# Queries projected transposed and placed by DMA, and score-maxima units moved among the routers, in a fused cross-attention and routed-FFN kernel

## The chip, the cores and the metric

The kernel runs on one core of a Trainium2 chip. The metric is the device time of one execution in microseconds (us), as the median of three runs; lower is better. PE is TensorE, DVE is VectorE, ACT is ScalarE, POOL is GpSimd and SP is SyncE, which issues most of the DMAs.

## The reference, cut to what matters

`x` is (4, 1024, 256), the context is (4, 154, 256), all in float32. With LN a layer norm without weights:

```
q = (LN(x) @ Wq.T + bq) * 16**-0.5     16 heads of 16 dims
k = ctx @ Wk.T + bk ; v = ctx @ Wv.T + bv
q, k = xpos(q), xpos(k)                pairs of dims rotated by position
x1 = x + tanh(g0) * (softmax(q k.T) v) @ Wo.T + bo   (bo inside the tanh factor)
h  = relu(mole(LN(x1), W1, b1, A1, B1, R1))          256 -> 1024
y  = x1 + tanh(g1) * mole(h, W2, b2, A2, B2, R2)     1024 -> 256
mole(x) = x @ W + b + 1/8 * sum over 3 experts of gate_e * (x @ A_e) @ B_e
gates   = softmax(x @ R)
```

The rotation turns each pair (x1, x2) of neighbouring dims into x1 cos - x2 sin and x2 cos + x1 sin.

## The kernel before, in words

**Steps.** The 4096 tokens are worked in 8 steps of 512 tokens (`CH`); step c covers half of one batch element, c = 2b + u. Each engine has its own program, written out by hand in `step`: steps 0 and 1 are special (`first`, `second`), steps 2 to 5 are a loop of two iterations, and steps 6 and 7 are written out again, with a tail behind them. The engines are kept together only by semaphores, and each works its own queue strictly in order. A step c works on three chunks of tokens at once: attention of c, the first FFN layer of d = c - 1, and the second FFN layer of e = c - 2. Steps 2 to 7, which hold all three, are called full.

**Number format.** Products that need full precision are made of float32r matmuls, with each operand split in a high and a low part and three products summed.

**Order of one full step on PE** (lines 1178 to 1258): the key operands if u is 0 (`key_transposes`, `project_v`); `out_tile` 0 and 1 of e (24 matmuls each, L1112); `project_out` of d (L988); `lora2_operand`, `out_tile` 2 and 3; `transpose_x`, which transposes the normalised rows of d into PSUM banks 2 and 3 of `psX` (L943); the first two groups of `q_transposes` of c (L1085); `lora2_operand` (L1122), `router1` of d (32 small matmuls, L1028), `out_lora` (L1128); then groups 2 to 7 of `q_transposes`, with `hidden_main(d, 0)` in two halves between them; `lora1_operand` (L1037), the transposed gated operand of layer one. Then come 16 units of `max_scores` (L1099, two matmuls of 308 columns each). Behind each of the first 13 stands half a `hidden_main` (three matmuls of 512 columns, L1052), and behind each second half the `hidden_lora` (L1058) that ends the sum of a hidden block of 128. After the tenth unit (i = 9) comes `max_transposed` (L1139). Last are 10 `scores` steps (L1155, L1158) with `values` (L1172, L1175), the transposes and `project_q` (L970) of c + 1 among them.

**Queries before.** `project_q` makes q with tokens on partitions: 24 matmuls of 256 columns. DVE adds the bias (`q_bias`, L646, 2 instructions), POOL multiplies by the cosines (L323), DVE by the sines (`q_sine`, L653, 4 instructions) and adds (`q_sum`, L661). ACT copies the high part twice into `split` (two 128x1024 copies), DVE subtracts it for the low part (`q_low`, L678). PE transposes 8 groups of two heads (32 transposes, 96 rows: high, low, high), and the groups are copied out of PSUM into `qT`, four by ACT and four by DVE (`q_transposed`, L721).

**The part around the maxima.** `reduce_max(c, i)` on DVE (L733) takes the maxima of unit i out of `psX`; unit i + 2 uses the same two banks, so `max_scores(c, i)` waits for reduction i - 2. `relu(d, m)` on ACT (L431) follows `hidden_lora(d, m)`, and `h_low(d, m)` on DVE (L726) follows `relu(d, m)`. There are three PSUM banks for hidden blocks, so `hidden_main(d, m)` waits for `h_low(d, m - 3)`. On ACT, `maxima_copy(c)` (L433 to L436) stands between `relu(d, 3)` and `relu(d, 4)`. It waits for `max_transposed(c, 0)`, which waits for eight reductions. `scores(c, 0)` waits for reduction 14. On DVE the order is two reductions, one `h_low`, and so on, so that ten reductions stand ahead of `h_low(d, 4)`:

```
for i in range(16):
    reduce_max(c, i)
    if not first:
        if i % 2:
            h_low(d, i // 2)
```

**Queues.** SP issues the loads at the start, and then only `rows_of_maxima`: four DMAs of 8 KB per step, from `split` into rows 96 and 97 of `qT`. ACT issues the x and context loads and the stores.

Of the kernel before, what the change touches and what calls it, by code (L numbers as in the profile page):

```python
# [65 lines left out]
def build(nc, x, ctx_in, wq, wkv, wo, w1, w2, a1, lora, tables, out):  # L66
    with ExitStack() as stack:
# [14 lines left out]
        split = sb("split", [P, TT * NG * KS], F32R)  # L82
        qs = split[:, :].rearrange("p (k g r) -> p k g r", k=TT, g=NG)
# [10 lines left out]
        q_ev = probs[:, 0:2, :].rearrange("p a (k e) -> p (a k) e", e=E)  # L94
        q_rc = probs[:, 2:4, :].rearrange("p a (k e) -> p (a k) e", e=E)
        q_rs = probs[:, 4:6, :].rearrange("p a (k e) -> p (a k) e", e=E)
# [18 lines left out]
        tab = sb("tab", [P, tables.shape[1]])  # L115
        ident_r = sb("ident_r", [P, P], F32R)
# [29 lines left out]
        cos_q = cols(UB * TT * D).rearrange("p (u k d) -> p u k d", u=UB, k=TT)  # L146
        sin_q = cols(UB * TT * D).rearrange("p (u k d) -> p u k d", u=UB, k=TT)
        cos_k = cols(2 * D).rearrange("p (a d) -> p a d", a=2)
        sin_k = cols(2 * D).rearrange("p (a d) -> p a d", a=2)
        bq_b, bk_b, bv_b, bo_b = cols(E), cols(E), cols(E), cols(E)  # L150
        g_b, mask = cols(2), cols(2)
# [34 lines left out]
        q_ps, q_evac = count("q_ps", 2), count("q_evac", 2)  # L186
        q_cos, q_sin, q_rot = count("q_cos", 1), count("q_sin", TT), count("q_rot", 1)
        q_hi, q_hi2, q_lo = count("q_hi", 1), count("q_hi2", 1), count("q_lo", 1)
        qT_ps, qT_a, qT_v = count("qT_ps", NG), count("qT_a", NG // 2), count("qT_v", NG // 2)
# [52 lines left out]
        def _(sp):  # L242
# [5 lines left out]
            stage("wq", wq)  # L248
            sp.dma_start(tab[:, :], tables).then_inc(tab_loaded.sem, 16)
# [13 lines left out]

            def rows_of_maxima(c):
# [7 lines left out]

            rows_of_maxima(0)
            rows_of_maxima(1)
            with sp.Fori(1, B) as b:
                rows_of_maxima(2 * b)
                rows_of_maxima(2 * b + 1)
# [3 lines left out]
        def _(pool):  # L281
# [37 lines left out]
            def step(b, u, first=False, last=False):  # L319
                c = 2 * b + u  # L320

                pool.wait_ge(q_evac.sem, q_evac.at(c))
# [31 lines left out]
        def _(act):  # L354
# [100 lines left out]
            def step(b, u, first=False, second=False, last=False):  # L455
# [5 lines left out]
                if first:  # L461
                    load(0, 1, 1)
                if u == 0:
                    key_operands(b)
# [6 lines left out]
                if not first:  # L471
                    act.wait_ge(wo_ps.sem, wo_ps.at(d))
# [908 lines left out]
```

## Time and profile before

| | us |
|---|---|
| median of 3 runs | 614.66 |
| lowest and highest run | 612.47, 615.61 |
| the profiled execution | 608.41 |
| its span, first to last instruction | 606.6 |
| mean granted TensorE clock | 0.946 |

The profile shows one execution. Busy times are the time in which an engine had an instruction in work. A group of instructions is named by the line that issues them, the tile written and the tile read. In a row of a timeline stand the start, the time from the first start to the last end, the engine, line and operation, the tiles and shapes, and in brackets how long the engine had been idle before it and who ended that.

The steps end, by the start of the next `project_q`, at 75.2, 141.5, 208.4, 275.0, 344.2, 410.9 and 477.5 us; what is behind step 7 begins at 543.5 us.

### The profile page before, as it was taken

Reading aid. Unit: us, or ns where it says so; the run is one execution under the profiler, and the core shown is the slowest. Engines: PE = TensorE matmul, PEld = TensorE weight load, DVE = VectorE, ACT = ScalarE, POOL = GpSimd, SP = SyncE. Lnnn points to the kernel's source line nnn. Section 1 sums busy time; section 2 is a strip of 40 time slices with the busy share of each in tenths; the row PEclk is TensorE's granted clock in tenths of the full one; section 3 lists DMA queues with packets and bytes.
Section 4 is the critical chain, followed back from the end, with each engine's and each line's share of the span. In section 5 each row is a group of like instructions: output and inputs, shape, how many; then the busy total and the mean of one; then the engine's idle time right before and its main releaser. Section 6 shows DMA issues by size and latency. Waiting matters only on the chain.

```text
span 606.6 us, 9214 instructions
## 1 busy us (share of the span) xinstructions
PE 527.2 (87%) x3360; PEld 400.8 (66%) x3360; DVE 415.7 (69%) x960; ACT 239.3 (39%) x389; POOL 84.8 (14%) x121
## 2 busy tenths in 40 slices
PE   2668965999989998999989998999899998989795
PEld 1545454856977497746876497747886597649574
DVE  4567356958887487956987487958897578644423
ACT  3252514453345424362445424362436343442210
POOL 2426012011100121011201121011201110101000
PEclk9865977999999998999999998999999999999798
DMA  8301000010001000010001010111001000100000
GB/s 263 111 2 36 2 35 2 1 47 27 11 2 72 1 36 2 36 47 10 31 1 72 1 36 2 41 42 37 1 1 71 1 2 1 71 1 1 1 36 35
DMA packets 6138, 18.57 MB, mean 31 GB/s; under 512 B 932, under 2 KB 1772, under 8 KB 5964
## 3 DMA queue, kind: packets, MB, share of 16 engines
q10 hardware_dynamic: 4005, 12.53, 5.8%
q1 hardware_dynamic: 2087, 5.42, 2.7%
q8 instruction: 29, 0.48, 0.3%
q14 instruction: 17, 0.14, 0.1%
HBM read 13.49 MB, written 4.19 MB: 29 GB/s over the span
## 4 chain that ended last, share of the span: by engine, by line
PE 68%; DVE 16%; ACT 7%; issue 6%; ACTq 1%; POOL 1%; DMA 1%; DVEq 0%
PE psF L1112 16%; PE psF L1052 11%; PE psX L1099 6%; ACT probs L521 5%; PE psX L1158 4%; DVE max_t L733 4%; PE psX L988 4%; PE psX L970 4%; PE psO L1172 3%; PE psO L1175 3%; PE psF L1172 3%; PE psF L1175 2%; PE psX L1085 2%; PE psF L1058 2%; PE psF L1028 1%
## 5 line engine op out<-in xcount | busy, mean ns | idle before, releaser
L733 DVE TENSOR_REDUCE max_t<-psX 128x4 fp32r<-128x616 f32 x128 | 99.5, 794 | 6.5 <-PE psX L1099 3.3
L521 ACT ACTIVATE probs<-psX 128x1024 f32<-128x1024 f32 x64 | 64.0, 1024 | 50.8 <-PE psX L1158 50.8
L1112 PE MATMUL psF<-w_hi,h_hi 128*128 128x284 f32 x256 | 76.8, 300 | 2.4 <-DVE h_lo L726 1.5
L1112 PE MATMUL psF<-w_lo,h_hi 128*128 128x284 f32 x256 | 75.1, 293 | 0.0
L1112 PE MATMUL psF<-w_hi,h_lo 128*128 128x284 f32 x256 | 74.9, 293 | 0.0
L1099 PE MATMUL psX<-km,qT 96*128 96x308 f32 x256 | 65.1, 341 | 6.9 <-DVE max_t L733 4.5
L1099 PEld LDWEIGHTS psX<-km,qT 96*128 96x128 f32 x256 | 48.6, 204 | 23.5 <-DVE max_t L733 12.8
L431 ACT ACTIVATE h_hi<-psF 128x512 fp32r<-128x512 f32 x64 | 37.3, 595 | 62.4 <-PE psF L1058 62.1
L726 DVE SCALAR_TENSOR_TENSOR h_lo<-psF,h_hi 128x512 fp32r<-128x512 f32 x64 | 43.7, 684 | 16.3 <-ACT h_hi L431 16.3
L1112 PEld LDWEIGHTS psF<-w_hi,h_hi 128*128 128x128 f32 x256 | 48.2, 188 | 7.9 <-issue 4.6
L1052 PE MATMUL psF<-xT_lo,w_hi 128*128 128x512 f32 x128 | 51.6, 414 | 0.0
L311 POOL TENSOR_TENSOR x<-x,tab 128x256 f32<-128x256 f32 x32 | 22.3, 730 | 206.4 <-DMA x<-in_x_dram 206.4
L1158 PE MATMUL psX<-qT,km 98*128 98x512 f32 x128 | 45.0, 447 | 4.6 <-ACT probs L521 4.1
L1112 PEld LDWEIGHTS psF<-w_hi,h_lo 128*128 128x128 f32 x256 | 48.2, 188 | 0.0
L1112 PEld LDWEIGHTS psF<-w_lo,h_hi 128*128 128x128 f32 x256 | 48.2, 188 | 0.0
L1052 PE MATMUL psF<-xT_hi,w_hi 128*128 128x512 f32 x128 | 42.8, 417 | 1.0 <-DVE zc L783 1.0
L1158 PEld LDWEIGHTS psX<-qT,km 98*128 98x128 f32 x128 | 20.5, 195 | 33.1 <-issue 17.2
L1052 PE MATMUL psF<-xT_hi,w_lo 128*128 128x512 f32 x128 | 40.6, 399 | 0.0
L757 DVE STREAM_TRANSPOSE heads_t<-psF 128x512 f32<-128x512 f32 x16 | 11.5, 717 | 38.5 <-PE psF L1175 33.8
L323 POOL TENSOR_TENSOR probs<-probs,tab 128x1024 f32<-128x1024 f32 x8 | 18.9, 2367 | 106.9 <-DVE probs L646 106.9
L1085 PE MATMUL psX<-ident_r,split 128*96 128x128 f32 x256 | 25.2, 253 | 4.9 <-DVE split L678 4.9
L356 ACT ACTIVATE split<-heads_t 128x512 fp32r<-128x512 f32 x16 | 10.0, 626 | 48.6 <-DVE heads_t L772 48.6
(155 smaller groups left out, 1003.4 us busy)
## 6 DMA issues: line engine op xcount, KB each, us to landing
x<-in_x_dram ACTq DMA_DIRECT2D x8, 512.0 KB, 3.3
x_ln<-in_x_dram ACTq DMA_DIRECT2D x7, 512.0 KB, 3.2
out_dram<-x ACTq DMA_DIRECT2D x7, 512.0 KB, 2.7
heads_t<-in_w_dram SPq DMA_DIRECT2D x1, 1024.0 KB, 8.3
heads_t<-in_w_dram SPq DMA_DIRECT2D x1, 994.0 KB, 4.7
tab<-in_tables_dram SPq DMA_DIRECT2D x1, 674.0 KB, 6.8
x_ln<-in_x_dram SPq DMA_DIRECT2D x1, 512.0 KB, 3.4
wkv_sb<-in_wkv_dram SPq DMA_DIRECT2D x1, 512.0 KB, 9.7
```

The lines of the kernel that those rows point to most:

```text
L431: nc.scalar.activation(h_hi[:, m, :], psF[:, (m + 1) % 3, :], ACT.Relu).then_inc(w1_hi_s.sem, 1)
L521: nc.scalar.activation(dst, psX[:, 2 * (i % 2):2 * (i % 2) + 2, :], ACT.Exp).then_inc(sc_exp.sem, 1)
L726: V.scalar_tensor_tensor(out=h_lo[:, m, :], in0=psF[:, (m + 1) % 3, :], scalar=0.0, in1=h_hi[:, m, :].bitcast(F32), op0=ALU.max, op1=ALU.s ...
L733: V.tensor_reduce(max_t[:, k, half, :].rearrange("p (h g) -> p g h", h=2)[:, 2 * j:2 * j + 2, :], psX[:, 2 * j:2 * j + 2, 0:2 * S].rearran ...
L970: ins = mm(o_ps, a[:, f, tokens(k)], w[:, f, :], start=n == 0, stop=n == 5)
L1052: mm(psF[:, (m + 1) % 3, :], w[:, f, P * m:P * m + P], a[:, f, :], start=n == 0, stop=False)
L1085: ins = nc.tensor.transpose(psX[0:KS, g % 4, tokens(k)].bitcast(F32R), qs[:, k, g, :], ident_r[:, :])
L1099: ins = mm(psX[:, g % 4, 0:2 * S], qT[0:KS, g, tokens(k)], km[0:KS, g, :, :].rearrange("p h s -> p (h s)"), start=True, stop=True)
L1112: ins = mm(psF[:, F_OF_K[k], 0:W2N], a[:, m, tokens(k)], w[:, m, :], start=m == 0 and i == 0, stop=m == HT - 1 and i == 2)
L1158: ins = mm(o_ps, km[:, n // 2, j, 0:P], qT[:, n // 2, :], start=True, stop=True)
L1172: mm(pv_bank(g), vr_sb[:, g, :], probs_r[:, g, :], start=True, stop=False)
L1175: ins = mm(pv_bank(g)[32 * j:32 * j + 32, :], v_sb[:, h, :], probs[:, h % 8, :], start=False, stop=True)
```

## The change

It does five things.

1. `project_q` swaps its operands: the weights are stationary, the tokens move. q comes out transposed, as two banks `psX[:, s, :]` of 128 rows by 512 tokens (12 matmuls of 512 columns). The weights are permuted so that bank 0 holds the first dim of each pair, bank 1 the second.
2. The rotation is done there. DVE makes four products with bias and table in one instruction each (`q_products`) and one difference and one sum of 128x512 (`q_turn`). ACT copies the high part (2 x 128x512) and DVE makes the low part (`q_low`, 2 x 128x512). POOL has no part in it any more. The tables of a half (512 KB) are loaded by SP for every step (`next_turn`).
3. Six DMAs of 256 KB per step on the SP queue put the rows in place in `qT`. They read 128 partitions by 2 KB and write 16 partitions by 16 KB. All PE transposes of q and the eight copies out of PSUM are gone.
4. The order of the maxima changes on PE and DVE, by `maxima_and_hidden`. In full steps unit 0 stands ahead of the router, unit 1 behind it, and the other 14 stand 2, 2, 2, 2, 3, 3 to the hidden blocks 2 to 7. Hidden blocks 0, 1 and 2 go ahead of `lora1_operand`. In step 1 six units go ahead of the transposes of x.
5. In step 0, `q_low` stands ahead of `key_operands`. On ACT the copies of the high part stand behind the first x load and ahead of `key_operands`.

```
+            def rows_of_queries(c):
+                for s in range(2):
+                    sp.wait_ge(q_hi.sem, q_hi.at(c, s + 1))
+                    for t in (0, 64):
+                        sp.dma_start(qT[t + 16 * s:t + 16 * s + 16, :, :].bitcast(F32),
+                                     probs[:, 4 + s, :]).then_inc(q_rows.sem, 16)
+                for s in range(2):
+                    sp.wait_ge(q_lo.sem, q_lo.at(c, s + 1))
+                    sp.dma_start(qT[32 + 16 * s:48 + 16 * s, :, :].bitcast(F32),
+                                 probs[:, s, :]).then_inc(q_rows.sem, 16)
+            def next_turn(c, u):
+                sp.wait_ge(q_prod.sem, q_prod.at(c))
+                sp.dma_start(turn[:, :, :], turns[u]).then_inc(turn_loaded.sem, 16)
...
+            def q_products(c):
+                dve.wait_ge(turn_loaded.sem, turn_loaded.at(c))
+                for s in range(2):
+                    dve.wait_ge(q_ps.sem, q_ps.at(c, s + 1))
+                    for dst, w in ((q_c, s), (q_s, 1 - s)):
+                        V.scalar_tensor_tensor(out=dst[:, w, :], in0=psX[:, s, :], scalar=bq_c[:, s:s + 1],
+                                               in1=turn[:, w ^ s, :], op0=ALU.add, op1=ALU.mult).then_inc(q_prod.sem, 1)
...
DVE, step:
-                for i in range(16):
-                    reduce_max(c, i)
-                    if first and i == 5:
-                        ln1_stats(c + 1)
-                    if not first:
-                        if i % 2:
-                            h_low(d, i // 2)
+                    n = MAX_AHEAD if second else 0
+                    for i in range(n):
+                        reduce_max(c, i)
                     x2T_low(d)
+                    reduce_max(c, n)
                     gates1_shift(d)
+                    reduce_max(c, n + 1)
+                    if full:
+                        finish(e, u, 2)
+                        finish(e, u, 3)
                     gates1_weigh(d)
+                    h_low(d, 0)
+                    h_low(d, 1)
+                    i = n + 2
+                    for m in range(2, HT):
+                        for _ in range(max_units(m, second)):
+                            reduce_max(c, i)
+                            i += 1
+                        h_low(d, m)
...
PE:
+            def maxima_and_hidden(c, d, e, full, second):
+                n = MAX_AHEAD if second else 0
+                if second:
+                    pe.wait_ge(x1_s.sem, x1_s.at(d))
+                    for i in range(n):
+                        max_scores(c, i)
+                    pe.wait_ge(max_red.sem, max_red.at(c, n))
+                transpose_x(d, psX[:, 2:4, :], ln2_out, x2T_ps)
+                pe.wait_ge(x1_s.sem, x1_s.at(d))
+                max_scores(c, n)
+                if full:
+                    lora2_operand(e, 1)
+                router1(d, second)
+                if full:
+                    out_lora(e, 1)
+                max_scores(c, n + 1)
+                for m in range(3):
+                    hidden_main(d, m, second)
+                lora1_operand(d)
+                hidden_lora(d, 0)
+                hidden_lora(d, 1)
+                i = n + 2
+                for m in range(2, HT):
+                    k = max_units(m, second)
+                    for part in range(2):
+                        for _ in range(k // 2 if part else k - k // 2):
+                            max_scores(c, i)
+                            if i == 9:
+                                max_transposed(c, 0, False)
+                            i += 1
+                        if m >= 3:
+                            hidden_main(d, m, second, (part,))
+                    hidden_lora(d, m)
...
+MAX_AHEAD = 6
+def max_units(m, second):
+    return ((0, 0, 1, 1, 1, 1, 2, 2) if second else (0, 0, 2, 2, 2, 2, 3, 3))[m]
```

The wait of `max_scores(c, 0)` is now for `q_rows`, all six DMAs; the order of `relu` and `maxima_copy` on ACT is as before.

## Rows read from the trace of the kernel before

**Rows 1.** Page, part 1: busy us and share of the span of each engine.
```profile
PE 527.2 (87%) x3360; PEld 400.8 (66%) x3360; DVE 415.7 (69%) x960; ACT 239.3 (39%) x389; POOL 84.8 (14%) x121
```

**Rows 2.** Busy time by stretch: PE, PEld, DVE, ACT, POOL, granted clock, DMA share, GB/s.
```profile
41.00:56.70 15.70, 13.47 (x37) 8.39 (x37) 13.95 (x26) 6.63 (x11) 11.88 (x11) 0.50 0.11 34
...
368.90:375.10 6.20, 6.15 (x69) 5.36 (x69) 4.56 (x16) 1.65 (x4) 0.00 (x0) 0.72 0.00 0
...
443.60:461.60 18.00, 17.23 (x88) 14.17 (x87) 16.84 (x26) 7.18 (x14) 0.00 (x0) 1.00 0.08 31
```

**Rows 3.** Groups by line with shapes kept apart: busy us, mean ns, idle before.
```profile
L1085 PE MATMUL psX<-ident_r,split 128*96 128x128 f32 x256 | 25.2, 253 | 4.9 <-DVE split L678 4.9
...
L721 DVE CAST qT<-psX 96x512 fp32r<-96x512 f32 x32 | 21.7, 680 | 4.3 <-PE psX L1085 4.3
...
L646 DVE TENSOR_TENSOR probs<-psX,tab 128x512 f32<-128x512 f32 x16 | 11.0, 688 | 3.7 <-PE psX L970 3.6
...
L678 DVE TENSOR_TENSOR split<-probs,split 128x1024 fp32r<-128x1024 f32 x8 | 9.7, 1210 | 0.0
```

**Rows 4.** Timeline of PE in step 6, from the x transposes to the scores.
```profile
436.11 0.77 PE L1085 MATMUL psX<-ident_r,split 128*96 128x128 f32 x8
...
438.82 0.64 PE L1028 MATMUL psF<-xT_hi,a_sb 128*32 128x128 f32 x16 [0.96 <-DVE xT_lo L639]
...
440.17 0.69 PE L1085 MATMUL psX<-ident_r,split 128*96 128x128 f32 x8
...
443.29 0.45 PE L1037 MATMUL psO<-ident_r,zs 128*96 128x128 f32 x4
...
445.22 0.39 PE L1058 MATMUL psF<-zT,lora_sb 96*128 96x512 f32 x1
445.45 0.45 PE L1099 MATMUL psX<-km,qT 96*128 96x308 f32 x2
445.74 0.40 PE L1052 MATMUL psF<-xT_lo,w_hi 128*128 128x512 f32 x1
...
454.55 0.41 PE L1139 MATMUL psO<-ident_r,max_t 128*8 128x128 f32 x4
...
461.61 0.49 PE L1155 MATMUL psX<-qT,kr 98*128 98x512 f32 x1
```

**Rows 5.** Timeline of DVE in step 6.
```profile
418.32 1.39 DVE L653 TENSOR_TENSOR probs<-probs,tab 128x256 f32<-128x256 f32 x4
...
437.39 1.28 DVE L639 TENSOR_TENSOR xT_lo<-psX,xT_hi 128x512 fp32r<-128x512 f32 x2
...
446.65 0.68 DVE L726 SCALAR_TENSOR_TENSOR h_lo<-psF,h_hi 128x512 fp32r<-128x512 f32 x1
...
456.09 0.69 DVE L726 SCALAR_TENSOR_TENSOR h_lo<-psF,h_hi 128x512 fp32r<-128x512 f32 x1 [0.54 <-ACT h_hi L431]
456.69 1.50 DVE L733 TENSOR_REDUCE max_t<-psX 128x4 fp32r<-128x616 f32 x2
```

**Rows 6.** Timeline of ACT in step 6.
```profile
443.77 0.59 ACT L356 ACTIVATE zT<-psO 96x512 fp32r<-96x512 f32 x1
445.65 0.60 ACT L431 ACTIVATE h_hi<-psF 128x512 fp32r<-128x512 f32 x1 [1.28 <-PE psF L1058]
...
454.99 0.59 ACT L356 ACTIVATE split<-psO 8x512 fp32r<-8x512 f32 x1 [3.11 <-PE psO L1139]
```

**Rows 7.** Timeline of DVE and PE in steps 0 and 1.
```profile
33.93 1.41 DVE L710 TENSOR_SCALAR km<-psX,tab 98x512 fp32r<-98x512 f32 x2
...
41.05 7.03 PE L1099 MATMUL psX<-km,qT 96*128 96x308 f32 x16
...
97.78 1.97 PE L943 MATMUL psX<-ident_r,xn 128*128 128x128 f32 x8 [7.55 <-ACT xn L411]
```

**Rows 8.** Page, part 6: DMA issues, KB each, median us from issue to landing.
```profile
x_ln<-in_x_dram ACTq DMA_DIRECT2D x7, 512.0 KB, 3.2
...
out_dram<-x ACTq DMA_DIRECT2D x2, 256.0 KB, 2.1
```

More of the change, by code:

```diff
@@ L63, in at, with build @@
         return self.per * n + (self.per if k is None else k)
-def build(nc, x, ctx_in, wq, wkv, wo, w1, w2, a1, lora, tables, out):
+def build(nc, x, ctx_in, wq, wkv, wo, w1, w2, a1, lora, tables, turns, out):
     with ExitStack() as stack:
@@ L271, in rows_of_maxima, with step @@
                                      max_f[4 * hh:4 * hh + 4, f, :].bitcast(F32)).then_inc(max_rows[f].sem, 16)
[L273 to L277, printed above, removed]
+            def step(b, u, last=False):
+                c = 2 * b + u
+                rows_of_queries(c)
+                if not last:
+                    next_turn(c, 1 - u)
+                rows_of_maxima(c)
+            step(0, 0)
+            step(0, 1)
+            with sp.Fori(1, B - 1) as b:
+                step(b, 0)
+                step(b, 1)
+            step(B - 1, 0)
+            step(B - 1, 1, last=True)
         @block.gpsimd
@@ L462, in step @@
                     load(0, 1, 1)
+                if not first:
+                    act.wait_ge(pv_ps.sem, pv_ps.at(d))
+                for s in range(2):
+                    act.wait_ge(q_rot.sem, q_rot.at(c, s + 1))
+                    copy(qh[:, s, :], q_c[:, s, :]).then_inc(q_hi.sem, 1)
                 if u == 0:
@@ L481, in step @@
                     x2T_high(d)
-                for g in range(0, NG, 2):
-                    act.wait_ge(qT_ps.sem, qT_ps.at(c, g + 1))
-                    copy(qT[0:KS, g, :], psX[0:KS, g % 4, :]).then_inc(qT_a.sem, 1)
-                    if full and g == 0:
-                        gate2_copy(e, 1)
-                    if not first and g == 0:
-                        gate1_exp(d)
+                if full:
+                    gate2_copy(e, 1)
                 if not first:
+                    gate1_exp(d)
                     gate1_copy(d)
@@ L822, in step @@
                     finish(e, u, 1)
-                q_low(c)
                 if full:
@@ L964, in project_q @@
                     pe.wait_ge(w_lo["wq"].sem, 1)
-                for k in range(TT):
-                    o_ps = psX[:, k // 2, E * (k % 2):E * (k % 2) + E]
+                for s in range(2):
                     n = 0
```

211 lines of the change are left out of this document (72 added, 139 removed).

## The prediction

> **What bounds the kernel now.** I read the page's busy shares first: PE is busy for 87% of the span, DVE for 69% [rows 1]. That names PE, but not the place. So I read the stretches next. From the first hidden blocks to the scores of step 6 PE is busy 17.23 of 18.0 us and DVE 16.84 of 18.0 [rows 2]: in the part that the change rebuilds, the two are full together, and neither can go faster without the other. That stretch stands in each of the six full steps. Third, the timelines of step 6. I set the clock to zero where DVE has finished the low part of the transposed x, at 437.39 + 1.28 = 438.67 us [rows 5], because the router waits for that and nothing ahead of it changes: up to there PE works on out tiles that the change doesn't touch. From that zero, before: router 0.15, gated operand 4.62, first `hidden_lora` 6.55, first scores 22.94 [rows 4], first `h_low` 7.98 [rows 5].
>
> **What leaves and what comes.** PE loses 256 transposes, 25.2 us busy in all, 3.15 a step [rows 3]. Its projection is 12 times 512 columns for 24 times 256, the same column count, so I cost it at nothing. DVE loses four casts of 680 ns a step, two bias sums of 688 and a low part of 1210 [rows 3], the four sine products (1.39 us) [rows 5] and one sum about as long as the low part. It gains four products, two halves of the turn and two of the low part. Priced as 128x512 rows, the four products are 4 x 0.69 = 2.8 us where the bias took 1.4; the turn and the low part are about 1.2 us each. The products fall between `project_q` and the last values of the step, where DVE waits for PE, and the turn takes the place of the sine products. So the DVE saving that lies on the path is the four casts, 2.5 us. POOL's cosines go; nobody was behind them. ACT's copies go; ACT has slack throughout. The new tables are fetched by a 512 KB load, 3.2 us [rows 8], a step early; the work that hides it is the whole step.
>
> **The rows' DMAs.** Six of 256 KB a step. No row here writes few partitions with that much. Bounds: below, half a 512 KB load, 1.6 us each or 9.6 us for six; above, 3.2 us each, a whole load, or 19.2 us [rows 8]. I take 2.1 us, the row of the 256 KB store [rows 8], since it also reads SBUF and has the same size: 12.6 us one behind the other. In step 6 the turn ends near 418.3 + 1.3 = 419.6 [rows 5]; the rows start at 420.2 and end at 432.8. Unit 0 is wanted where the q transposes were, at 436.1 [rows 4]. So in full steps they cost nothing; their cover is PE's out tiles, 16 us of them, and beyond that all PE work stops behind unit 0, which now stands ahead of the router.
>
> The Trainium skill, SBUF — State Buffer, Door 1: The DMA port swizzle, says that a transfer's rate goes with the ports its partitions reach, and that partitions 0 to 15 reach four of sixteen, measured at 104 GB/s. By it a 256 KB piece would take an estimated 2.5 us and six 15 us, and the sum below would be about 6 us higher. No run here shows it yet. It also speaks against this change, since each piece writes 16 partitions.
>
> **A full step, after.** I follow the new queues from the same zero.
> - Router to 1.5, with its lora product behind it (PE is free for the next at 440.17 [rows 4]). Unit 1 takes 0.29, the step from 445.45 to 445.74 [rows 4]. Then three hidden blocks stand ahead of the gated operand: 18 matmuls of 0.23, the step from 445.22 to 445.45 [rows 4], 4.2 us. The operand comes at 6.0, against 4.62.
> - ACT's copy starts 0.48 after it and lasts 0.59 [rows 4, 6], so the first `hidden_lora` is at 7.1; relu 0.43 behind that, `h_low` 0.63 later: 8.2 against 7.98. The removed transposes have bought nothing by here, because what the gates wait for is no longer filled by them but by hidden work, and DVE stands idle from about 5.0, when its gates are done.
> - From the first `h_low` to the scores, before, 14.96 us. DVE's own work in it is 13 reductions of 0.70 (two take 1.50 with an overlap, 1.50 - 0.80 [rows 5]) and 7 `h_low` of 0.60 (from 456.09 to 456.69 [rows 5]), 13.3 us. The same 13 and 7 stand there after: only units 0 and 1 were done earlier, and they were before, too. So this stretch has no saving at all, only new gaps:
>  - `h_low(4)`. It waits for relu 4, that for `maxima_copy`, that for the maxima's transposes, those for the eighth reduction. From those transposes to the `h_low` is 456.09 - 454.55 = 1.54 us [rows 4, 5]. Before, ten reductions stood ahead of it, so two (1.4 us) filled the wait and 0.54 was left [rows 5]. After, eight stand ahead: none fills it. The eighth ends, PE finishes the half block in front (0.3) and unit 9 (0.3), then 1.54: a gap of 2.2. Price 1.7.
>  - Blocks 6 and 7 have three units each. The middle of each block now waits for a reduction of its own group, and `hidden_lora` and relu follow: 0.8 at `h_low(6)`, 0.5 at `h_low(3)`.
>  - At the end, unit 15 waits for reduction 13, and half a block (0.7) and its `hidden_lora` (0.2) stand between it and the scores: 0.6 more than before.
> - So 14.96 becomes 17.6 less the rounding of these, scores at 8.2 + 17.6 = 25.8, against 22.94: **2.9 us slower** a full step. Behind the scores the queues are as they were.
> - In two of the six steps the clock was down in the stretch behind the router (0.72, and 6.2 us for what takes 5 elsewhere [rows 2]). There 18 big matmuls now stand instead of 6, so I add 0.3 for each of two steps.
>
> Six full steps: 6 x 2.9 + 0.6 = +18.0.
>
> **Step 0.** Before, the maxima begin at 41.05 [rows 7]. After, `q_low` comes ahead of the key operands that began at 33.93 [rows 7], and ends at 35.2; the two low pieces take 4.2, so they land at 39.5: -1.5. (Bounds 38.4 and 41.6, so -2.7 to +0.6.) Loading the tables costs at the start: 512 KB in the SP queue ahead of the weights, hidden, since PE waits for the layer norm there.
>
> **Step 1.** Six units go ahead of the x transposes of 97.78, where PE had been idle for 7.55 us [rows 7]. A unit takes 0.88 there (16 matmuls, 8 units in 7.03 [rows 7]), 5.3 us. The rows start near 84 and land at 96.5; units to 102.3; transposes 4.5 late. Behind it six reductions less (4.2), given back by 1.2 where the first `h_low` comes later: -3.0. Sum +1.5. With the lower bound of the rows it is -1.
>
> **Sum.** 18.0 - 1.5 + 1.5 = +18.0: a span of 624.6 for 606.6, a profiled execution of 626.4 for 608.41. The profiled execution stands 6.2 us below the median of the runs, 614.66, so against that: 614.66 + 18.0 = **632.7 us**, 2.9% slower.
>
> **Rivals.**
> - *The gaps don't open, and the casts and transposes come off.* This needs DVE to be the pace with PE always ahead of it. For it: 16.84 of 18.0 busy [rows 2]. Then each full step gains its four casts, 2.5 us, steps 0 and 1 gain 1.5 and 1: 614.66 - 17.5 = 597; all PE transposes gone is the floor, 589.5. It decides when the first `h_low` comes by 5.5 from zero and the one at block 4 has no gap. Against it: the order of ACT and the eight reductions. Chance 0.22.
> - *Partly filled.* The gaps only eat the saving: 612 to 618. Chance 0.08.
> - *Rows late.* From 13.5 us for six, unit 0 holds up PE's queue. At 2.5 us each, between the row taken and the upper bound: step 0 +1.4 instead of -1.5, step 1 +3.9 more than at 2.1 less 1.5, i.e. +2.4, full steps 0.2 each: about +6, 639. At 3.2 each about 4 us a full step, 660. The mechanism is that each piece writes only 16 partitions, unlike every row above. Chance 0.22, the larger because nothing like it is in this trace. (The rule of the Trainium skill's page named above is this one.)
> - *The clock falls in the maxima.* In step 0, with maxima alone, PE is 13.47 of 15.7 busy and the clock stays at 0.50 [rows 2]. After, PE has gaps in the same stretch of each full step. At half clock its 36 big matmuls and 14 units take some 7 us more: 675. Against it, they are mixed with full-sized matmuls. Chance 0.05.
> - The forecast keeps 0.43.
>
> **The numbers.** Half a per cent, 3 us, is about what a measurement of this kernel can tell from no change. Faster 0.22 (the first rival), within it 0.08, slower 0.70. The range takes in most of the first rival above its floor and the rows at 2.5 us with room for a little more: 598 to 645. The forecast alone would be 624 to 639.
>
> **What would show it.** In the changed profile: first `h_low` of a full step near 8.2 us after the low part of x; an idle time of about 2.2 us ahead of the fifth `h_low`, ended by ACT; scores at 25 to 26; DVE idle time in front of L-lines of `h_low` of 6 us a step instead of 1 to 2. The rows: `max_scores` of unit 0 directly behind the x transposes, with no wait on a DMA. I am wrong if a full step from zero to the scores takes 21 us or less, and wrong on the DMAs if PE's idle time is ended by `qT` landing.

## The result

The changed kernel takes **656.55 us** (median of 4 runs, 653.22 to 661.54) against 615.08 us of the kernel before in the same comparison. The two medians are 6.7% apart; the ratio over the runs is 1.0714, 95% interval 1.0637 to 1.0791. That is about 7% slower, where 2.9% was forecast and 645 us was the end of the range. The profiled execution took 661.54 us with a span of 659.7, against 608.41 and 606.6 before; its mean granted clock is 0.900, before 0.946. It is the slowest of its four runs, and the profiled execution of before lies 6.2 us under its median. So the two profiles are 53.1 us apart and the medians 41.5. Sums of stretches below hold for the two profiled executions, and make the loss look about 12 us larger than a run in the middle has it.

The page of the changed kernel, busy time by engine, against [rows 1]:

```profile
PE 536.8 (81%) x3008; PEld 394.6 (60%) x3008; DVE 398.3 (60%) x928; ACT 214.7 (33%) x357; POOL 64.7 (10%) x113
```

PE has 352 instructions fewer: the 256 transposes, and 96 because the projection streams the same columns in half as many matmuls. The transposes alone were 25.2 us of work [rows 3], and yet PE is busy 9.6 us longer. So the matmuls that stayed take longer. DVE has lost 17.4 us of work, and its share has gone from 69% to 60%: it waits more. Two questions, then: where PE waits, and where its clock is.

The stretches from zero (the end of the low part of the transposed x) to the first scores, steps 2 to 7 of the changed kernel; columns as in [rows 2]:

```profile
178.40:207.40 29.00, 23.71 (x128) 18.59 (x129) 18.82 (x36) 7.25 (x14) 0.00 (x0) 0.88 0.05 19
247.50:279.40 31.90, 26.77 (x132) 21.33 (x133) 18.97 (x36) 7.63 (x15) 0.00 (x0) 0.79 0.06 21
329.90:361.40 31.50, 26.09 (x128) 20.99 (x129) 18.83 (x36) 7.25 (x14) 0.00 (x0) 0.78 0.05 18
401.50:433.10 31.60, 25.88 (x133) 20.32 (x134) 18.90 (x36) 7.64 (x15) 0.00 (x0) 0.84 0.08 29
479.10:508.30 29.20, 24.04 (x129) 18.66 (x130) 18.74 (x35) 7.16 (x14) 0.00 (x0) 0.88 0.05 19
548.20:579.20 31.00, 25.88 (x132) 20.16 (x133) 18.88 (x35) 5.58 (x11) 0.00 (x0) 0.83 0.05 18
sum 184.20, PE 152.37 PEld 120.05 DVE 113.14 ACT 42.50 POOL 0.00; mean PE 25.40 PEld 20.01 DVE 18.86 ACT 7.08 POOL 0.00
```

The same six stretches before, those of steps 3 and 6 and the sum of all six:

```profile
232.80:256.80 24.00, 23.35 (x155) 19.43 (x155) 20.71 (x40) 9.07 (x17) 0.00 (x0) 0.93 0.06 23
...
438.70:461.60 22.90, 22.01 (x154) 18.38 (x155) 20.59 (x39) 8.86 (x17) 0.00 (x0) 1.00 0.06 24
...
sum 140.10, PE 134.84 PEld 112.54 DVE 124.00 ACT 51.77 POOL 0.00; mean PE 22.47 PEld 18.76 DVE 20.67 ACT 8.63 POOL 0.00
```

So 44.1 of the 53.1 us by which the spans differ lie in these six stretches (184.2 less 140.1), and they have two parts. PE is idle for 31.8 us (184.2 - 152.4) instead of 5.3. And it is busy for 17.5 us more, though 144 transposes are gone from these stretches (24 in each; the other eight of a step stood ahead of zero). The column behind POOL's, the granted clock, says why: 0.78 to 0.88 in the six, against 1.00 in four of the six before and 0.93 in the other two.

How both look in step 2. DVE of the changed kernel, from the first `h_low`:

```profile
186.77 1.29 DVE L728 SCALAR_TENSOR_TENSOR h_lo<-psF,h_hi 128x512 fp32r<-128x512 f32 x2 [3.33 <-ACT h_hi L451]
...
192.55 0.69 DVE L728 SCALAR_TENSOR_TENSOR h_lo<-psF,h_hi 128x512 fp32r<-128x512 f32 x1 [1.07 <-ACT h_hi L451]
...
194.15 0.80 DVE L735 TENSOR_REDUCE max_t<-psX 128x4 fp32r<-128x616 f32 x1 [0.19 <-PE psX L1087]
197.92 0.69 DVE L728 SCALAR_TENSOR_TENSOR h_lo<-psF,h_hi 128x512 fp32r<-128x512 f32 x1 [2.97 <-ACT h_hi L451]
```

and PE over the same time:

```profile
188.82 0.56 PE L1087 MATMUL psX<-km,qT 96*128 96x308 f32 x2 [1.69 <-DVE max_t L735]
...
196.13 0.41 PE L1127 MATMUL psO<-ident_r,max_t 128*8 128x128 f32 x4
...
196.66 0.62 PE L1058 MATMUL psF<-xT_hi,w_lo 128*128 128x512 f32 x2
197.12 0.40 PE L1064 MATMUL psF<-zT,lora_sb 96*128 96x512 f32 x1
199.37 0.55 PE L1087 MATMUL psX<-km,qT 96*128 96x308 f32 x2 [1.85 <-DVE max_t L735]
...
202.48 1.05 PE L1058 MATMUL psF<-xT_hi,w_lo 128*128 128x512 f32 x2
```

PE runs dry twice. The first `h_low` comes late and DVE's reductions behind it, so PE waits 1.69 us at 188.82. Then the eighth reduction ends at 194.95. The transposes of the maxima follow at 196.13, ACT's copy and relu behind them, and DVE stands 2.97 us in front of the fifth `h_low`. With it stand the next reductions, so PE waits again: 1.85 us ahead of unit 10. A little later two hidden matmuls take 1.05 us where two took 0.62. The clock in that place, in stretches of 2 us of the same kernel:

```profile
188.00:190.00 2.00, 1.18 (x6) 1.05 (x7) 2.00 (x5) 0.00 (x0) 0.00 (x0) 1.00 0.00 0
190.00:192.00 2.00, 2.00 (x9) 1.66 (x8) 1.48 (x3) 0.08 (x1) 0.00 (x0) 0.62 0.04 8
192.00:194.00 2.00, 2.00 (x8) 1.71 (x8) 1.40 (x2) 0.52 (x1) 0.00 (x0) 0.53 0.02 4
...
198.00:200.00 2.00, 0.55 (x2) 0.30 (x2) 2.00 (x4) 2.00 (x5) 0.00 (x0) 1.00 0.52 203
200.00:202.00 2.00, 1.92 (x7) 1.52 (x8) 2.00 (x4) 0.33 (x1) 0.00 (x0) 0.68 0.00 0
202.00:204.00 2.00, 2.00 (x7) 1.61 (x6) 0.83 (x2) 0.00 (x0) 0.00 (x0) 0.50 0.00 0
```

From 198 to 200 PE is busy only 0.55 of 2 us; the next 2 us show 0.68, and the 2 us behind them 0.50, the 1.2 GHz level. The spell at 190 to 194 also follows a wait: PE is busy 1.32, 1.13 and 1.18 of 2 us in the three stretches from 184 on. Both losses in the step come in this order: a wait, then slow matmuls. Step 6 has two such spells as well, and steps 3, 4, 5 and 7 have three. In these five steps the first lies right behind the router, in front of which PE has waited for the low part of x or for the rows. The kernel before has only this kind, and only in steps 3 and 5.

Steps 0 and 1 lost too. Two entries of the chain that ended last, changed kernel:

```profile
37.13 6.83 DMA qT<-probs
...
89.75 12.86 DMA qT<-probs
```

In step 0 the rows land at 43.96 (37.13 + 6.83), the scores start at 59.6 instead of 56.7: +2.9. In step 1 they land at 102.6, six units follow, and zero comes at 112.1 instead of 101.1; of these 11.0 us step 0 had brought 2.9. Its stretch to the scores then takes 20.3 instead of 22.2.

### The profile page after: what moved, and what is told of

The parts are those of the page before. It is cut to its first block, busy times and chain, and to the rows that moved or that the text cites. A ratio compares the mean times of both kernels' runs of the same rounds, so it can differ in the third digit from the quotient of the medians.

```text
span 659.7 us, 8444 instructions
## 1 busy us (share of the span) xinstructions
PE 536.8 (81%) x3008; PEld 394.6 (60%) x3008; DVE 398.3 (60%) x928; ACT 214.7 (33%) x357; POOL 64.7 (10%) x113
## 4 chain that ended last, share of the span: by engine, by line
PE 59%; DVE 14%; DMA 9%; ACT 9%; issue 5%; SPq 2%; ACTq 1%; POOL 0%; DVEq 0%
PE psF L1058 15%; PE psF L1100 10%; DMA qT<-probs 8%; PE psX L1087 6%; ACT probs L536 5%; DVE max_t L735 4%; PE psX L1146 4%; PE psO L1160 3%; PE psO L1163 2%; PE psF L1064 2%; PE psX L977 2%; PE psF L1160 2%; ACT h_hi L451 2%; DVE probs L663 2%; PE psF L1034 2%
## 5 line engine op out<-in xcount | busy, mean ns | idle before, releaser
L1087 PE MATMUL psX<-km,qT 96*128 96x308 f32 x256 | 73.5, 392 | 59.1 <-DMA qT<-probs 29.6
L735 DVE TENSOR_REDUCE max_t<-psX 128x4 fp32r<-128x616 f32 x128 | 97.5, 794 | 24.6 <-PE psX L1087 24.6
L1087 PEld LDWEIGHTS psX<-km,qT 96*128 96x128 f32 x256 | 54.1, 241 | 83.7 <-DVE max_t L735 45.6
L1058 PE MATMUL psF<-xT_hi,w_hi 128*128 128x512 f32 x128 | 48.0, 461 | 1.2 <-DVE zc L785 1.1
L1058 PE MATMUL psF<-xT_hi,w_lo 128*128 128x512 f32 x128 | 45.2, 438 | 0.0
L376 ACT ACTIVATE zT<-psO 96x256 fp32r<-96x256 f32 (+1 forms) x24 | 10.8, 451 | 69.3 <-PE psO L1043 38.0
L1058 PEld LDWEIGHTS psF<-xT_lo,w_hi 128*128 128x128 f32 x128 | 28.4, 222 | 5.3
L1064 PE MATMUL psF<-zT,lora_sb 96*128 96x512 f32 x64 | 26.9, 441 | 5.5 <-ACT zT L376 5.5
L1058 PEld LDWEIGHTS psF<-xT_hi,w_lo 128*128 128x128 f32 x128 | 27.4, 214 | 4.8
```

Source lines behind the costliest of these rows:

```text
L735: V.tensor_reduce(max_t[:, k, half, :].rearrange("p (h g) -> p g h", h=2)[:, 2 * j:2 * j + 2, :], psX[:, 2 * j:2 * j + 2, 0:2 * S].rearran ...
L1058: mm(psF[:, (m + 1) % 3, :], w[:, f, P * m:P * m + P], a[:, f, :], start=n == 0, stop=False)
L1064: mm(psF[:, (m + 1) % 3, :], lora_sb[:, P * m:P * m + P], zT[:, :], start=False, stop=True).then_inc(w1_ps.sem, 1)
L1087: ins = mm(psX[:, g % 4, 0:2 * S], qT[0:KS, g, tokens(k)], km[0:KS, g, :, :].rearrange("p h s -> p (h s)"), start=True, stop=True)
```

## The experiments

Each kernel was timed beside the kernel before, whose median was 614.19, 614.38 and 614.36 us in the three groups.

**1. The order alone.** The new projection, rotation and rows stay; PE's and DVE's queues stand in the order of before, with the transposes and casts of q left out. The first loop is PE's, behind `hidden_main(d, 0)` and `lora1_operand`, the second DVE's, behind the gates and `finish`.

```diff
+                for i in range(16):
+                    max_scores(c, i)
...
+                    if i < 13:
+                        m = i // 2 + 1
+                        hidden_main(d, m, second, (i % 2,))
...
+                    for i in range(16):
+                        reduce_max(c, i)
+                        if i % 2:
+                            h_low(d, i // 2)
```

> The changed kernel with the order of maxima and hidden blocks of the kernel before (units in pairs with h_low, one half block behind each unit, no units ahead in step 1); queries still transposed and placed by DMA. Theory A, the new order and the clock that its PE gaps cost are most of the loss: from the low part of x to the scores a full step takes 21 to 24 us (29 to 32 in the changed kernel, 23 to 24 before), the granted clock there is 0.93 or more, and the median is 608 to 622. Theory B, the DMA traffic or the transposed queries slow the steps by themselves: the stretch stays near 30 us and the median above 640.

Measured: 605.79 us (604.47 to 608.14), ratio 0.9883, interval 0.9834 to 0.9933. The changed kernel's new order costs 50.8 us, and the rest of the change gains 8.4, a little over 1%. Its stretches:

```profile
172.10:194.00 21.90, 20.66 (x131) 16.65 (x131) 18.39 (x36) 7.32 (x14) 0.00 (x0) 1.00 0.07 26
...
437.40:459.90 22.50, 21.77 (x131) 17.81 (x131) 18.38 (x36) 7.23 (x14) 0.00 (x0) 0.93 0.06 25
...
sum 132.90, PE 127.27 PEld 103.35 DVE 110.26 ACT 41.89 POOL 0.00; mean PE 21.21 PEld 17.22 DVE 18.38 ACT 6.98 POOL 0.00
```

This splits the loss in the profiled executions. The same work takes 51.3 us less (184.2 - 132.9): 25.1 us of it are PE's busy time (152.4 - 127.3), the lower clock, and 26.2 are its idle time (31.8 - 5.6). About half and half. The clock's rows fit: in steps 3, 4 and 6 here there is one spell below 1.00, right behind the router, and in steps 2, 5 and 7 none. The spells in the middle of the stretch are gone with the waits there. About 8 us of the idle time that went are PE's waits for the rows ahead of the router in steps 3, 5 and 7 (2.31, 2.90 and 2.74), since unit 0 no longer stands there; experiment 4 shows that they were not worth that much.

**2. The gap at the fifth h_low.** ACT's copy of the maxima, and the store with it, behind relu 5.

```diff
-                        if m == 3:
+                        if m == 5:
                             maxima_copy(c)
```

> The changed kernel with one move on ACT: the copy of the maxima stands behind relu 5 and not behind relu 3. Theory A: the gap in front of the fifth h_low (3 us of DVE idle in the changed kernel) closes, and some of the lost clock with it: 2.5 to 4 us a full step, median 632 to 642. Rival: the gap is only shifted to the next wait of the chain and the median stays within 4 us of 656.

Measured: 641.83 us (639.45 to 646.33), ratio 1.0445 (1.0392 to 1.0498). One wait taken out of ACT's queue gives back 14.7 us. In the profiled execution the six stretches take 15.0 us less, 169.2, of which 8.8 are PE's busy time; 5.4 of these 8.8 fell in one step. Step 4 happened to run at full clock throughout, although PE waited in it too. It shows how long the order takes without slow matmuls: 24.8 us, with no wait in front of the fifth `h_low` and 0.56 us at the sixth.

```profile
326.90:351.70 24.80, 20.72 (x129) 16.24 (x130) 18.75 (x35) 7.25 (x14) 0.00 (x0) 1.00 0.06 23
...
467.70:495.20 27.50, 23.40 (x128) 18.76 (x129) 18.77 (x35) 7.25 (x14) 0.00 (x0) 0.88 0.05 21
```

The two steps run the same instructions. At 0.88 they take 2.7 us longer, and that is all in PE's busy time.

**3. Filling the gap with work for the clock.** Eleven extra 512-column matmuls a full step, into a bank that nobody reads then; the outputs don't change.

```diff
+                extra = {2: 5, 4: 6}
...
                     hidden_lora(d, m)
+                    if full:
+                        for _ in range(extra.get(m, 0)):
+                            mm(psO[:, :], w1_hi[:, 0, 0:P], xT_hi[:, 0, :], start=True, stop=True)
```

> The changed kernel with work added that nobody reads: in full steps five matmuls of 512 columns behind the hidden_lora of block 2 and six behind that of block 4, where PE otherwise waits for a reduction. The outputs do not change. Theory clock: PE stays at the upper level, granted clock 0.95 or more in the stretch instead of 0.78 to 0.88, and the time falls although work is added, by 2 to 4 us a full step, median 632 to 645. Rival, the gaps alone make the loss and the clock is a bystander: no change, or up to 10 us slower.

Measured: 655.48 us (654.11 to 657.51), the same as the changed kernel. The clock in the stretches rose to 0.89 to 0.94, from 0.78 to 0.88, and the steps still took 28.9 to 31.2 us. The two places did different things. The first filler stands in a wait: PE's 1.69 us behind block 2 became 1.31 us of filler and a wait of 0.55. And the slow spell behind it is gone, in all six steps:

```profile
190.00:192.00 2.00, 2.00 (x12) 1.70 (x11) 1.53 (x3) 0.60 (x1) 0.00 (x0) 1.00 0.03 8
192.00:194.00 2.00, 2.00 (x11) 1.64 (x10) 1.70 (x3) 0.00 (x0) 0.00 (x0) 1.00 0.01 4
```

The fourth `h_low` then waited 0.47 us in step 2 instead of 1.07. That ties this spell to the wait. The second filler missed its place: it stands behind block 4, where PE did not wait, and the wait of 1.85 us behind block 5 stayed, in step 2 with the slow matmuls behind it. Its 1.4 us stood ahead of the transposes of the maxima, and the fifth `h_low` waited longer:

```profile
197.42 0.69 DVE L728 SCALAR_TENSOR_TENSOR h_lo<-psF,h_hi 128x512 fp32r<-128x512 f32 x1 [3.72 <-ACT h_hi L451]
```

In step 2 the fourth `h_low` came 0.55 us earlier than in the changed kernel and the fifth only 0.10, so the second filler took most of what the first had won. Work that stands in a queue where it did not wait costs its own length; what filler in both waits would have given was not run.

**4. A third less to land.** From step 1 on only four of the six pieces are sent; rows 64 to 95 keep step 0's values, so the products with the second copy of the high part are those of step 0.

```diff
-                    for t in (0, 64):
+                    for t in ((0, 64) if first else (0,)):
```

> The changed kernel, but from step 1 on only four of the six row DMAs are issued: rows 64 to 95 (the second copy of the high part) keep what step 0 put there, so the products with the low part of k use old rows. Theory rows: the four land in 10 us instead of 15, step 1 gains 5 us, steps 3, 5 and 7 gain 1 to 2.5 each, median 645 to 650. Rival, the rows are hidden in all steps but the first: within 3 us of 656.

Measured: 655.77 us (652.72 to 659.1), no change against 656.55. Zero of step 1 came at 106.8 instead of 112.1, and the waits of steps 3, 5 and 7 ahead of the router were gone. The full steps then took 29.2 to 31.6 us, and these three together 94.3 instead of 94.5. Their clock was 0.78, so they lost the waits and not the slow matmuls. Whatever the two pieces cost in steps 1 to 7, it is under the scatter of the medians.

**5. The gated operand earlier.** Only its place in PE's queue.

```diff
-                for m in range(3):
-                    hidden_main(d, m, second)
+                hidden_main(d, 0, second)
                 lora1_operand(d)
+                for m in range(1, 3):
+                    hidden_main(d, m, second)
```

> The changed kernel with the gated operand's transposes (lora1_operand) behind the first hidden block instead of the third; nothing else moves. Queue theory: the first h_low of a full step comes 1.2-1.6 us earlier (7 us from zero instead of 8.3-9.7), the gap ahead of the fifth h_low stays at 2.5-3.5, so the scores come about 1.3 us earlier in each of six steps: 656.5 - 8 = 648 us. Rival 1 (the clock decides): the gap at block 4 still lets the granted clock fall in the second half of the stretch, and the median stays within 3 us of 656.5. Rival 2 (the early operand is worth nothing, DVE is the pace behind it): same number as rival 1, but with DVE's idle time moved to just behind the first h_low.

Measured: 663.92 us (662.5 to 664.63), ratio 1.0825 (1.0772 to 1.0879): 7 us slower than the changed kernel, against 8 faster expected. The profiled executions don't show these 7 us: 662.5 us at a mean clock of 0.901 here, 661.54 at 0.900 there, and the six stretches take 182.5 us here and 184.2 there. The other runs of the changed kernel had 0.904 to 0.913, those of this one 0.896 to 0.899. So what the medians differ by goes with the clock, and where it is lost is open. Why nothing was won, the start of the stretch shows. PE in step 4 of this kernel:

```profile
332.83 0.63 PE L1058 MATMUL psF<-xT_hi,w_lo 128*128 128x512 f32 x2
335.18 0.47 PE L1043 MATMUL psO<-ident_r,zs 128*96 128x128 f32 x4 [1.72 <-DVE zs L629]
335.49 1.02 PE L1058 MATMUL psF<-xT_hi,w_hi 128*128 128x512 f32 x2
...
339.90 0.63 PE L1064 MATMUL psF<-zT,lora_sb 96*128 96x512 f32 x2
```

The operand came 2.4 us earlier (5.05 from zero instead of 7.44). But two hidden blocks now stand between it and the first `hidden_lora`, and PE had to wait 1.72 for the gates, behind which two matmuls took 1.02 us where two had taken 0.63. `hidden_lora` came at 9.77 instead of 8.53, and the first `h_low` at 10.8 instead of 9.7. I had said that the blocks delay the operand. They fill a wait that is there anyway; the first `h_low` goes by all that stands in front of the first `hidden_lora`.

**6. No units ahead in step 1.**

```diff
-MAX_AHEAD = 6
+MAX_AHEAD = 0
```

with a full step's distribution of the units in step 1 as well.

> The changed kernel with no units of step 1 ahead of its x transposes: step 1 is ordered as a full step. If the rows' transfers and the six units hold step 1 up, zero of step 1 comes at 102-104 us (112.1 changed, 101.1 before, 102.8 in e1). What stands against it is that zero to scores of step 1 grows from 20.3 to about 27-29. Forecast: the two cancel, median 655-658; the six units ahead are worth nothing while the rows land as late as they do. If instead the units ahead were a gain, it is 2-5 us slower.

Measured: 659.17 us (655.18 to 660.73). Zero of step 1 came at 103.5, its stretch took 27.8 us, and the scores came at 131.3 instead of 132.4. The six units ahead are worth nothing that shows, as expected.

**7. A second queue for the rows.** The two pieces for rows 64 to 95 are issued by ACT.

```diff
+                for s in range(2):
+                    act.wait_ge(q_hi.sem, q_hi.at(c, s + 1))
+                    nc.scalar.dma_start(qT[64 + 16 * s:80 + 16 * s, :, :].bitcast(F32),
+                                        probs[:, 4 + s, :]).then_inc(q_rows.sem, 16)
```

> The changed kernel with the two pieces of the high part that go to rows 64 to 95 issued from ACT's queue, the other four from SP's. If the rate is set by the queue (one after the other in SP's), six pieces take about 10 us instead of 15.2, zero of step 1 comes near 107 as in e4_four_pieces (106.8), and steps 3, 5, 7 have no wait ahead of the router. [...] The median is expected at 654-658 in both, since e4 has shown that the rows' time is given back.

Measured: 657.24 us (654.4 to 658.17). While the rows run, this kernel moves 135 GB/s and the changed one 129, the last column of these two, with all 16 DMA engines busy (the share is over 1):

```profile
235.00:243.00 8.00, 8.00 (x64) 7.81 (x63) 6.38 (x28) 2.46 (x5) 2.92 (x7) 1.00 1.10 135
```

```profile
235.00:243.00 8.00, 8.00 (x66) 8.00 (x66) 7.16 (x31) 1.65 (x5) 1.64 (x5) 1.00 1.08 129
```

So the queue is not what sets the rate, or only a little of it. Zero of step 1 came at 108.4, 3.7 us earlier. 1.7 of that is an earlier start: the first issue in step 1 is at 84.67 instead of 86.37. From there to the landing the six pieces took 14.3 us instead of 16.2, where about 10 were expected of two queues if one queue were the limit.

**8. The table's load out of the way.** In the changed kernel here, and on top of experiment 10 in experiment 11.

```diff
                 rows_of_queries(c)
-                if not last:
-                    next_turn(c, 1 - u)
                 rows_of_maxima(c)
+                if not last:
+                    next_turn(c, 1 - u)
```

> The changed kernel with the table's load issued behind the rows of the maxima, nothing else. Contention theory: the rows land 3-4 us earlier, zero of step 1 at 108 instead of 112.1, no wait for the rows ahead of the router in steps 3, 5, 7, and, as with four pieces, little of it is left in the end: 650-656. Rival (the rows alone set the landing): 656, zero of step 1 at 112.

Measured: 658.47 us (656.07 to 660.63), zero of step 1 at 111.6. No effect: in this kernel the table's load is not what makes the rows late, as the rival had it.

**9. The rows' transfer by itself.** On top of experiment 10: copies of the rows' form, behind the last w2 matmul.

```diff
+            for t, p in group:
+                sp.dma_start(t[p:p + 16, :, :].bitcast(F32), turn[:, 0, :]).then_inc(probe.sem, 16)
...
+            sp.dma_start(h_lo[:, j, :].bitcast(F32), turn[:, 0, :]).then_inc(probe.sem, 16)
```

> f1_filled with copies added behind its last w2 matmul, from a 128x512 tile to h_hi and h_lo, one group after another, each waited for: a piece of 16 partitions x 16 KB as the rows' (rows 0); two (rows 0 and 64); two (0 and 32); two (0 and 16); six (0 to 95); then 1, 2 and 6 copies of the same 256 KB to all 128 partitions. The outputs are unchanged, the time at the end is longer. If the ports set the rate (the Trainium skill, SBUF page, on the ports: 0-15 and 32-47 share four, 16-31 and 64-79 have others): one piece about 2.5 us and a fixed part, 0+64 and 0+16 no longer than one, 0+32 twice one, six about 5 us, and the full-width copies 1.3 us each. If it is a rate of the whole of these transfers, as the 105 to 145 GB/s with all 16 DMA engines busy looks: every two cost twice one whatever their rows, six cost 12 to 15 us, and full-width copies are at least twice as fast. If neither (SBUF to SBUF copies are slow whatever they write), the full-width copies are as slow as the narrow ones.

Measured in one profiled execution, 642.72 us with the copies. The rows are stretches as in [rows 2], in order: pieces to rows 0 and 32; to 0 and 16; six to rows 0 to 95; then six copies of the same 256 KB to all 128 partitions. The single piece and the pair 0 and 64 ran beside the output's last stores and are not used.

```profile
602.50:606.50 4.00, 0.00 (x0) 0.00 (x0) 0.00 (x0) 0.00 (x0) 0.00 (x0) 0.50 0.96 131
609.00:613.00 4.00, 0.00 (x0) 0.00 (x0) 0.00 (x0) 0.00 (x0) 0.00 (x0) 0.50 0.91 131
615.00:628.50 13.50, 0.00 (x0) 0.00 (x0) 0.00 (x0) 0.00 (x0) 0.00 (x0) 0.50 0.97 117
...
635.50:640.50 5.00, 0.00 (x0) 0.00 (x0) 0.00 (x0) 0.00 (x0) 0.00 (x0) 0.50 0.84 315
```

Bytes and the share of busy DMA give the rate. Six narrow pieces: 117 x 13.5 = 1.58 MB in 0.97 x 13.5 = 13.1 us of full use, 120 GB/s or 2.2 us a piece. Six wide copies: 315 x 5 = 1.58 MB in 4.2 us, 375 GB/s, 0.7 us each. The same bytes from the same tile cost three times as much when 16 partitions are written instead of 128.

**10. Filling the waits of experiment 1.** Four moves on top of it: unit 0 ahead of the first hidden block and unit 1 ahead of the gated operand; reduction 0 between the halves of the gates and reductions 1 and 2 ahead of the first `h_low`, so that eleven stand ahead of the fifth; the copy of the maxima behind relu 4; in step 0 the high and low parts ahead of the next x load and the values' bias.

```diff
+                max_scores(c, 0)
                 hidden_main(d, 0, second)
+                max_scores(c, 1)
                 lora1_operand(d)
...
                     gates1_shift(d)
+                    reduce_max(c, 0)
                     gates1_weigh(d)
...
-                        if m == 3:
+                        if m == 4:
                             maxima_copy(c)
```

> The changed kernel in the order of the kernel before (as e1_old_order), with four moves: unit 0 of the maxima stands between out_lora and the first hidden block and unit 1 ahead of the gated operand, where PE waited 0.8 us in e1; reduction 0 goes between the two halves of the gates and reductions 1 and 2 ahead of the first h_low, where DVE waited 0.6, 0.4 and 0.6 us; the copy of the maxima stands behind relu 4 instead of relu 3; in step 0 the high copies and q_low go ahead of the next x load and the bias of the values. Queue theory: zero to scores falls from 21.5-22.5 us in e1 to about 20.5 in a full step, six times 1.3 is 8 us, step 0 gives 1-2 more: 596 us. Rival (the clock decides): PE is as full as in e1 and no more, steps with the lower clock in the stretch stay at 22, and the median is 602-606.

Measured: 597.95 us (595.15 to 599.03), ratio 0.9732 (0.9692 to 0.9773): faster than both kernels, 2.7% under the one before. Its stretches:

```profile
169.20:191.90 22.70, 22.56 (x131) 19.04 (x132) 18.47 (x35) 7.31 (x14) 0.00 (x0) 0.86 0.06 25
...
432.80:453.50 20.70, 19.93 (x130) 16.67 (x131) 18.30 (x35) 7.31 (x14) 0.00 (x0) 1.00 0.07 27
...
sum 130.40, PE 128.94 PEld 108.76 DVE 110.42 ACT 42.02 POOL 0.00; mean PE 21.49 PEld 18.13 DVE 18.40 ACT 7.00 POOL 0.00
```

PE is idle for 1.5 us of 130.4. The stretches are only 2.5 us shorter than in experiment 1, though: 4.2 us less idle, 1.7 more busy. Against experiment 1 the clock is lower in three of them and higher in one; the step with 1.00 takes 20.7, the two with 0.86 take 22.7. Each theory holds in a part, the queue's in the idle time and the clock's in the busy time. The spans differ by 5.4 us, and the other 2.9 lie ahead of the scores of step 1. In step 0 the rows were issued 6 to 9 us earlier and landed at about the same time (43.6 instead of 44.1).

**11. The same with the table's load late.**

> f1_filled with the 512 KB load of the next table (turn) issued behind the rows of the maxima instead of directly behind the six pieces of the rows. In f1 the rows of step 0 were issued at 22.5 to 28.5 us and landed only at 43.77, with the table and the next x load under way at the same time. Contention theory: without the table's 512 KB, at the 105 to 145 GB/s seen, they land about 4 us earlier, 39.5-40.5, step 1's rows too, and steps 2 to 7 don't change; median 598 - 4 to 6 = 593. Rival (the rows alone set the landing, by how few partitions they write): landing at 43 and the median within 2 us of 598.

Measured: 597.66 us (595.58 to 599.01). Step 0's maxima begin at 40.4 instead of 43.8, zero of step 1 comes 1.8 us earlier, at 99.3, and the median does not move. In the changed kernel (experiment 8) the same edit had moved step 0 by nothing. One difference is when it is issued: in experiment 10 at 28.52, 15.1 us ahead of the landing, in the changed kernel at 37.72, 6.2 us ahead. Whether that is the reason stays open.

## Why the prediction was wrong in size

The direction and its reason held, and the time did not.

- **The part I priced as a gain** (casts and transposes off, rows hidden in full steps) is one: 8.4 us by experiment 1. That is half of the 17.5 that the first rival gave it (and its four casts are 2.7 us a step by the 21.7 of [rows 3], where I wrote 2.5). As a forecast this rival failed because the gaps did open.
- **First h_low at 8.2.** At full clock it came at 8.34 (step 2). In steps 4 and 6 it came at 9.7, in the odd steps at 10.1 to 10.9. In step 4 the clock was down in the stretch behind the router, where 18 hidden matmuls stand instead of six:

```profile
330.00:337.50 7.50, 7.43 (x57) 6.19 (x57) 4.13 (x14) 0.21 (x1) 0.00 (x0) 0.77 0.00 0
```

- **The gap at h_low(4), 2.2.** Measured 2.97 in step 2 and 2.3 to 3.0 in the others. ACT ends it, as said. Its price of 1.7 a step was too low: experiment 2 took it out and won 14.7 us, 2.4 a step.
- **Scores at 25.8.** The sum has a flaw of its own. Its terms are 1.7, 0.8, 0.5 and 0.6, and 14.96 with them is 18.6; I wrote 17.6 "less the rounding", which takes 1.0 us off each step without a reason. At full clock the one step seen (experiment 2, without the gap) took 24.8. The terms as they stand, less 1.7 for the gap, give 25.1, and the written 25.8 less 1.7 gives 24.1. So the walk at full clock was sound to under 1 us. The changed kernel's steps took 29.0 to 31.9, 30.7 in the mean. The **step that failed** is the clock's term. I gave it 0.3 us for each of two steps, and to the clock falling in the maxima a chance of 0.05. Experiment 1 puts it at 25 us over the six steps, half of what the order cost in the profiled executions. It is also in the waits: in front of the fourth `h_low` I had 0.5, the step at full clock shows 0.47, and the changed kernel 1.06 to 1.53. My ground against it was that full-sized matmuls are mixed in, which says nothing of the waits between them: I had worked out waits of about 3 us and then priced the matmuls behind them at full speed. The row that should have warned me stood in [rows 2]: 0.72 behind the router, in a stretch that PE enters from a wait. That a wait brings the spell is shown for the place behind block 2, by the first filler of experiment 3; elsewhere it is read from what stands before each spell.
- **Rows' DMAs, 2.1 us a piece.** By itself a piece takes 2.2 (experiment 9). But in step 3 of the changed kernel six of them took 15.2 us, from the first issue to the landing at 247.43:

```profile
232.22 2.83 SPq L267 DMA_DIRECT2D qT<-probs  x4
235.09 1.68 SPq L271 DMA_DIRECT2D qT<-probs  x2
```

  The next x was loading beside the first of them. Unit 0 waited for them in steps 3, 5 and 7, which the forecast had excluded; PE's waits for them are 29.6 us in five places:

```profile
PE psX L1087 <- DMA qT<-probs: 29.6, 5, 10.9
```

  So the third rival is right as a mechanism. In the full steps it shows nothing in the time (experiment 4), and steps 0 and 1 came out at +2.9 for -1.5 and at +6.2 for +1.5 (8.1 less 1.9, to the scores of step 1). In step 0 the forecast let only the two low pieces follow `q_low`, 4.2 us. But the four high ones were issued from 28.45 on, the last low one at 37.7, and the landing came 6.3 us behind it. In step 1 my 96.5 and 5.3 make 101.8, where I wrote 102.3; the rows landed at 102.6.
- The Trainium skill, SBUF — State Buffer, Door 1: The DMA port swizzle, gave 104 GB/s and an estimated 15 us for six. The 120 GB/s of narrow pieces against 375 GB/s of wide ones agrees with it in kind, and is somewhat above its figure: six took 13.1 us by themselves, and 15.2 with a load beside them. Its other half, that rows 0 to 15 and 16 to 31 reach different ports, showed no use for two separate pieces in one queue: they took 3.6 us of full use, and rows 0 and 32, which share ports, 3.8 (131 GB/s over 4 us in both).

The sums of the profiled executions: in the six full steps +18.0 was forecast and +44.1 measured, and the 26 between them are about what experiment 1 shows of the clock; in steps 0 and 1 nothing was forecast (-1.5 and +1.5) and +9.1 measured. By the medians the loss is 41.5, so in a run in the middle the clock's part is smaller than these 26. How much smaller, no profile shows. Of the 50.8 us that the order costs, only ACT's wait is separated by a run (14.7). Which of its other parts opens the other waits, the three blocks ahead of the operand or the new spread of the units, was not taken apart.

## What to carry to other kernels

When two engines feed each other, write down for each wait in the new order how much work stands ahead of it in the waiting queue: eight reductions instead of ten opened the gap here. Price a wait on TensorE twice: its own length, and the matmuls behind it at the lower clock if a row of the kernel shows the clock falling already. Count the waits before the stretch as well. Before giving up a change, run it in the old order: here the rewrite was a gain of 1.2%, and of 2.7% once the waits were filled, hidden behind an order that cost 8%.

## What was not expected of the hardware

- The grant falls behind a wait, for the most part: in the stretch where PE was busy for 0.55 of 2 us it still read 1.00, and in the next two 0.68 and 0.50, with PE busy for 1.92 and 2.00. PE's waits there were under 2 us.
- A kernel with PE idle for 1.1% of its maxima (experiment 10) still had 0.86 to 0.92 in five of six steps. In all five the low rows lie in the first 8 us of the stretch, behind PE's waits ahead of the router; nothing falls later. In its step 2:

```profile
167.00:169.00 2.00, 0.34 (x2) 0.19 (x2) 1.87 (x7) 0.95 (x3) 0.00 (x0) 0.93 0.14 47
169.00:171.00 2.00, 1.66 (x32) 1.51 (x32) 0.19 (x1) 0.00 (x0) 0.00 (x0) 0.50 0.00 0
```

  Such a wait doesn't always bring it. Step 2 of experiment 1 has the same 0.34 and no spell, and what decides between the two stays open:

```profile
170.00:172.00 2.00, 0.34 (x2) 0.20 (x2) 1.90 (x7) 0.86 (x2) 0.00 (x0) 1.00 0.07 16
172.00:174.00 2.00, 1.75 (x35) 1.38 (x36) 0.65 (x4) 0.00 (x0) 0.00 (x0) 1.00 0.00 0
```

- Writing 256 KB to 16 partitions ran at 120 GB/s with all 16 DMA engines counted busy, to 128 partitions at 375 GB/s. A second queue raised 129 GB/s to 135 only.
